# Audio tower on one core: second feed-forward with its down projection two inner blocks behind gate and up, and the token mixer's score order moved by one

## The reference

```
h = mixer(x)                        # 128 sequences of 512, 32 channels: softmax(q k) v
h = h + attention(layernorm(h))     # a0: rotary positions, 32 heads of 16
h = h + ternary_ffn(layernorm(h))   # f0: silu(x w1) * (x w3), w2, weights in {-s, 0, s}
h = h + attention(layernorm(h))     # a1: alibi slopes, 16 heads of 32
h = h + fp4_ffn(layernorm(h))       # f1, the stage that the change is about
```

```
gate, up = x @ w_gu          # 512 -> 2 x 1408; a scale for each output and 128 inputs
h = silu(gate) * up
y = h @ w_down               # 1408 -> 512
out = y / sqrt(mean(y*y) + 1e-6)
```

## Time and profile before

| | |
|---|---|
| median of 3 runs (lowest to highest) | 2395.11 us (2394.86 to 2395.63) |
| profiled execution: its own time | 2391.57 us |
| its span, first to last instruction | 2389.8 us |
| granted TensorE clock over the span | 0.985 |
| PE busy | 2244.2 us, 94% of the span |
| DVE / ACT / POOL busy | 1662.7 / 1495.3 / 1021.4 us |

### The profile page before, as it was taken

One profiled execution on the slowest core, in us unless ns is written; L12 is line 12 of the kernel. 1 busy time (PEld: TensorE's weight loads), 2 busy tenths in 40 slices (PEclk: granted clock), 3 DMA queues, 4 the chain that ended last, 5 costly groups with the idle time before them and its releaser, 6 DMA issues. The chain is left out here.

```text
span 2389.8 us, 41107 instructions
## 1 busy us (share of the span) xinstructions
PE 2244.2 (94%) x13188; PEld 1128.5 (47%) x13188; DVE 1662.7 (70%) x2931; ACT 1495.3 (63%) x2398; POOL 1021.4 (43%) x1007
## 2 busy tenths in 40 slices
PE   6999999998999996799999999999987999999998
PEld 2333333335666663344444445666652444444443
DVE  6666666665888887456667634666657888888873
ACT  4666666666788785355656425667745666667663
POOL 1222222237777773223324302444434555555552
PEclk9999999999999998799999999999999999999999
DMA  5545445442343211312223212222221011111101
GB/s 146 138 127 135 129 127 135 130 110 66 111 131 114 67 58 36 109 50 79 80 89 93 67 48 84 80 79 79 79 67 40 23 49 40 53 41 45 45 27 53
DMA packets 144300, 194.94 MB, mean 82 GB/s; under 512 B 32773, under 2 KB 76261, under 8 KB 144154
## 3 DMA queue, kind: packets, MB, share of 16 engines
q1 hardware_dynamic: 115642, 154.79, 21.7%
q10 hardware_dynamic: 28512, 38.28, 5.7%
HBM read 125.10 MB, written 42.21 MB: 70 GB/s over the span
## 5 line engine op out<-in xcount | busy, mean ns | idle before, releaser
L341 DVE TENSOR_REDUCE tm_negmax<-tm_s 128x1 f32<-128x512 f32 x512 | 323.3, 679 | 164.7 <-PE tm_s L384 164.4
L303 ACT ACTIVATE tm_prob<-tm_s 128x1024 f32<-128x1024 f32 x256 | 257.6, 1023 | 136.9 <-PE tm_s L404 130.6
L2119 PE MATMUL f_part<-f_xhi,gu 128*128 128x512 f16 x704 | 269.4, 383 | 17.8 <-ACT f_firstg L1922 6.3
L2119 PE MATMUL f_part<-f_xlo,gu 128*128 128x512 f16 x704 | 268.6, 382 | 0.0
L421 PE MATMUL tm_o<-tm_prob,tm_vt 128*64 128x512 f32 x1024 | 255.7, 620 | 0.0
L1888 POOL TENSOR_TENSOR f_firstg<-f_firstg,f_secondg 128x512 f32<-128x512 f32 x88 | 150.7, 1712 | 193.3 <-DVE f_secondg L2006 193.3
L2141 PE MATMUL f_pz<-dn,f_ghi 128*128 128x512 f16 x704 | 214.5, 380 | 5.9 <-ACT f_zc L1954 5.9
L384 PE MATMUL tm_s<-tm_qk 96*128 96x512 f16 x512 | 199.2, 391 | 14.6 <-DMA tm_qk<-tm_xs 14.1
L264 POOL TENSOR_TENSOR tm_hn<-tm_nd,tm_rows 128x1024 f32<-128x1024 f32 x32 | 75.3, 2353 | 291.8 <-DMA tm_rows<-rden 291.8
L404 PE MATMUL tm_s<-tm_qk 98*128 98x512 f16 x512 | 194.2, 382 | 1.6 <-DMA tm_qk<-tm_mrow 1.6
L975 PE MATMUL a_bankB<-a_wo,a_yThi 128*128 128x512 f16 x512 | 158.7, 393 | 4.1 <-DVE a_yTlo L899 4.0
(11 more groups left out here) (190 smaller groups left out, 5668.4 us busy)
## 6 DMA issues: line engine op xcount, KB each, us to landing
tm_qk<-tm_xs SPq DMA_DIRECT2D x384, 64.0 KB, 2.1
tm_xqk<-in_qk ACTq DMA_DIRECT2D x32, 512.0 KB, 4.3
a_hin<-h SPq DMA_DIRECT2D x64, 256.0 KB, 2.7
a_hres<-h SPq DMA_DIRECT2D x64, 256.0 KB, 3.0
h<-a_hout SPq DMA_DIRECT2D x64, 256.0 KB, 2.5
f_hin<-h SPq DMA_DIRECT2D x64, 256.0 KB, 2.7
f_hres<-h SPq DMA_DIRECT2D x64, 256.0 KB, 2.8
tm_vt<-in_vt ACTq DMA_DIRECT2D x32, 256.0 KB, 3.0
```

The source lines that it names most:

```text
L303: nc.scalar.activation(prob[b][:, 2 * h:2 * h + 2, :], s2[:, i % 2, :, :], ACT.Exp, scale=SCALE).then_inc(exp_done, 1)
L341: nc.vector.tensor_reduce(negmax[u][:, m:m + 1], s1[:, p % BANKS, :], AX.X, ALU.max, negate=True).then_inc(s1_read, 1)
L2119: last = nc.tensor.matmul(part[q % BANKS][:, :], (gate, up)[which][:, j, m * P:(m + 1) * P], xparts[x][u][:, j, :], start=x == 0, stop=x == 1)
```

## The change

In the second feed-forward the down projection of a block runs two blocks behind it (`LAG = 2`), in the same step, with its 12 matmuls spread one and two at a time behind the 8 products. Four sums, one for each tile of the group, stay open in four PSUM banks (`pz` becomes a list). Products and transposes share the other four banks in turn (`turn`, `bank_of`, `wait_bank`) where there were six and one. `ghi` and `glo` become rings of 4 blocks. The last two blocks of a group are projected in the first two blocks of the next step, so there are 9 steps where there were 10. The four sums are copied out together in blocks 1 and 2. `hidden` and `hidden_lo` of a group's last block move into the next step's first block.

The float16 halves of `xn` are made before the transposes: ACT `x_high`, POOL `x_low`, then PE makes 8 float16 transposes into one bank, and one ACT copy (`copy_x`, 1024 float16 values a partition) takes both halves out. DVE's `x_lo` goes. In the mixer `LEAD` becomes 15, and the transposes move by one use of the banks, so that one more matmul for maxima stands between the eighth maximum and the transpose that needs it.

The core of the diff (the renaming of arguments, the loops that call `step_u`, and what only follows from these are left out):

```diff
-    LEAD = 14
+    LEAD = 15
-        return 0 if m == 0 else m + 1 if m < 9 else m + 2
+        return m if m < 2 else m + 1 if m < 10 else m + 2
-        return 1 if pair else 10
+        return 2 if pair else 11
...
-    BANKS = 6
-    xn = sb("xn", [P, DM], F32)
-    xhi, xlo = pair("xhi", [P, KT, GT], F16), pair("xlo", [P, KT, GT], F16)
+    xn, halves = sb("xn", [P, DM], F32), sb("halves", [P, 2, DM], F16)
+    xs = pair("xs", [P, 2, KT, GT], F16)
     act_out, prod = pair("act_out", [P, GT], F32), pair("prod", [P, GT], F32)
-    ghi, glo = pair("ghi", [P, MT, GT], F16), pair("glo", [P, MT, GT], F16)
+    RING = 4
+    ghi, glo = sb("ghi", [P, RING, GT], F16), sb("glo", [P, RING, GT], F16)
-    zc, square = [extra_sb(f"zc{i}", [P, DM], F32) for i in range(2)], extra_sb("square", [P, DM], F32)
+    zc, square = [extra_sb(f"zc{i}", [P, DM], F32) for i in range(NT)], extra_sb("square", [P, DM], F32)
-    part5, pz, px = (ps(n, [P, GT], F32) for n in ("part5", "pz", "px"))
-    part = [ps(f"part{i}", [P, GT], F32) for i in range(BANKS - 1)] + [part5]
+    bank = [ps(f"bank{i}", [P, GT], F32) for i in range(8)]
+    turn = [bank[i] for i in (3, 4, 5, 2)]
+    pz = [bank[i] for i in (6, 7, 0, 1)]
+    pz_free = [before.done[n] for n in ("y_done", "y_done", "yTlo_done", "out_done")]
...
-    down_to = {0: (0, 0, 6), 1: (0, 6, 12), 2: (0, 12, 18), 3: (0, 18, 23), 4: (0, 23, 28), 5: (0, 28, 33),
...
-    out_at = {9: (1, 0), 14: (1, 1), 20: (1, 2), 3: (2, 3)}
+    squares_at = [3, 5, 7, 8]
+    mean_at = [4, 6, 8, 9]
+    out_at = [5, 7, 9, 10]
+    LAG = 2
+    uses = []
+    for m in range(MT):
+        uses += [(m, i) for i in range(8)]
+        if m in norm_at:
+            uses.append((None, norm_at.index(m)))
+    assert len(uses) % 4 == 0
+    def bank_of(m, i):
+        return turn[uses.index((m, i)) % 4]
+    def wait_bank(pe, g, m, i):
+        at = len(uses) * g + uses.index((m, i)) - 4
+        if at >= 0 and uses[at % len(uses)][0] is None and at // len(uses) == GROUPS - 1:
+            at -= 4
+        if at < 0:
+            return
+        back, (m, i) = at // len(uses), uses[at % len(uses)]
+        if m is None:
+            pe.wait_ge(s["xs_done"], NT * (back + 1) + i + 1)
+        else:
+            pe.wait_ge(s[("scale_done", "join_done")[i % 2]], 4 * (MT * back + m) + i // 2 + 1)
...
-        def step(k, u):
-            n = 2 * k + u
-            store(n - 2, 2)
+        def step(n):
             residual(n - 1, 0)
-            store(n - 2, 3)
             residual(n - 1, 1)
             load(n + 1, 2)
             load(n + 1, 3)
@@ -1856,6 +1878,8 @@
             store(n - 1, 1)
             residual(n - 1, 3)
             load(n + 2, 1)
+            store(n - 1, 2)
+            store(n - 1, 3)
         return normalise, step
...
+        def x_low(g, i):
+            if inside(g, GROUPS):
+                t = NT * g + i
+                wait(pool, s["high_done"], t + 1)
+                wait(pool, s["xT_ready"], t)
+                pool.tensor_tensor(halves[:, 1, :], xn[:, :], halves[:, 0, :], ALU.subtract).then_inc(s["low_done"], 1)
...
+            if i >= 0:
+                x_low(0, i)
...
+                sum_parts(n, m, 0)
+                if m + 1 in norm_at:
+                    x_low(n + 1, norm_at.index(m + 1))
+                if m in mean_at:
+                    inverse_rms(n - 1, mean_at.index(m))
+                sum_parts(n, m, 1)
                 if m + 3 in norm_at:
                     inverse_deviation(n + 1, norm_at.index(m + 3))
...
         def normalise(i):
-            x_hi(0, i, 0)
-        def scale_part(g, m, u, which, j):
+            if i:
+                copy_x(0, i - 1, 0)
+            if i < NT:
+                x_high(0, i)
...
+        def hidden_hi(g, m):
+            if inside(g, GROUPS):
+                n = MT * g + m
+                wait(act, s["prod_done"], n + 1)
+                wait(act, s["part_ready"], 8 * (n - 1))
+                nc.scalar.copy(ghi[:, n % RING, :], prod[n % 2][:, :]).then_inc(s["ghi_done"], 1)
+        def x_high(g, i):
+            if inside(g, GROUPS):
+                t = NT * g + i
+                wait(act, s["xn_done"], t + 1)
+                wait(act, s["xT_ready"], t)
+                nc.scalar.copy(halves[:, 0, :], xn[:, :]).then_inc(s["high_done"], 1)
+        def copy_x(g, i, u):
+            if inside(g, GROUPS):
+                px = (bank_of(None, i) if g else turn[3])[:, :].bitcast(F16)
                 wait(act, s["xT_ready"], NT * g + i + 1)
                 if i == 0:
                     wait(act, s["part_ready"], 8 * MT * (g - 1))
-                nc.scalar.copy(xhi[u][:, :, i * P:(i + 1) * P], px[:, :].rearrange("p (j n) -> p j n", j=KT))\
-                    .then_inc(s["xhi_done"], 1)
+                nc.scalar.copy(xs[u][:, :, :, i * P:(i + 1) * P].rearrange("p x j n -> p (x j) n"),
+                               px.rearrange("p (n c) -> p n c", c=P)).then_inc(s["xs_done"], 1)
...
-                wait(act, s["out_done"], t - 1)
-                nc.scalar.copy(zc[i % 2][:, :], pz[:, :]).then_inc(s["zc_done"], 1)
+                wait(act, s["out_done"], t + 1 - NT)
+                nc.scalar.copy(zc[i][:, :], pz[i][:, :]).then_inc(s["zc_done"], 1)
...
-        def step(k, u):
-            n = 2 * k + u
+        def step(n):
             for m in range(MT):
-                for which in range(2):
-                    at = 2 * m + which
-                    if at in copied_at:
-                        back, i = copied_at[at]
-                        z_out(n - back, i)
-                    scale_part(n, m, u, which, 0)
-                    if at in copied_at:
-                        squares(n - back, i)
-                    scale_part(n, m, u, which, 2)
-                    if which == 0 and m:
-                        hidden_hi(n, m - 1, u)
-                gate_act(n, m, u)
-                if m in norm_at:
-                    x_hi(n + 1, norm_at.index(m), 1 - u)
-            z_out(n - 1, 3)
-            squares(n - 1, 3)
-            hidden_hi(n, MT - 1, u)
+                if m - 1 in norm_at:
+                    copy_x(n + 1, norm_at.index(m - 1), (n + 1) % 2)
+                scale_part(n, m, 0, 0)
+                if m == LAG:
+                    z_out(n - 1, 3)
+                scale_part(n, m, 0, 2)
+                hidden_hi(*((n, m - 1) if m else (n - 1, MT - 1)))
+                if m == LAG - 1:
+                    z_out(n - 1, 0)
+                scale_part(n, m, 1, 0)
+                if m == LAG - 1:
+                    z_out(n - 1, 1)
+                if m + 1 in norm_at:
+                    x_high(n + 1, norm_at.index(m + 1))
+                if m in squares_at:
+                    squares(n - 1, squares_at.index(m))
+                scale_part(n, m, 1, 2)
+                if m == LAG - 1:
+                    z_out(n - 1, 2)
+                gate_act(n, m)
...
-                wait(dve, s["xT_ready"], t)
+                wait(dve, s["low_done"], t)
-        def x_lo(g, i, u):
-            if inside(g, GROUPS):
-                wait(dve, s["xhi_done"], NT * g + i + 1)
-                nc.vector.tensor_tensor(xlo[u][:, :, i * P:(i + 1) * P], px[:, :].rearrange("p (j n) -> p j n", j=KT),
-                                        xhi[u][:, :, i * P:(i + 1) * P], ALU.subtract).then_inc(s["xlo_done"], 1)
...
+                before = (n, m - 1) if m else (n - 1, MT - 1)
+                join_part(n, m, 0, 1)
+                hidden(*before)
+                join_part(n, m, 0, 3)
+                hidden_lo(*before)
+                if m in mean_at:
+                    mean_square(n - 1, mean_at.index(m))
+                join_part(n, m, 1, 1)
+                if m + 2 in norm_at:
+                    x_normalised(n + 1, norm_at.index(m + 2))
+                join_part(n, m, 1, 3)
+                if m in out_at:
+                    output(n - 1, out_at.index(m))
                 if m + 3 in norm_at:
-                    i = norm_at.index(m + 3)
-                    row_stats(n + 1, i, 2 * (n + 1) + i // 2)
-            hidden(n, MT - 1, u)
-            hidden_lo(n, MT - 1, u)
+                    row_stats(n + 1, norm_at.index(m + 3))
...
+        def products_of(g, m, which, j):
+            if inside(g, GROUPS):
+                i = 4 * which + j
+                if m == 0 and i == 0:
+                    wait(pe, s["xs_done"], NT * (g + 1))
+                wait_bank(pe, g, m, i)
+                for x in range(2):
+                    last = nc.tensor.matmul(bank_of(m, i)[:, :], (gate, up)[which][:, j, m * P:(m + 1) * P],
+                                            xs[g % 2][:, x, j, :], start=x == 0, stop=x == 1)
+                last.then_inc(s["part_ready"], 1)
+        def transpose_x(g, i):
+            if inside(g, GROUPS):
+                t = NT * g + i
+                px = (bank_of(None, i) if g else turn[3])[:, :].bitcast(F16)
+                wait(pe, s["low_done"], t + 1)
```

(43 more changed lines are left out.)

159 lines of the change are left out of this document (52 added, 107 removed), and 3 rows, old and new, of the table down_to.

## The result

The changed kernel takes 2355.93 us (median of 4 runs, 2354.9 to 2361.06) where the kernel before, beside it, takes 2395.14: a ratio of 0.984, 95% interval 0.9823 to 0.9857. Its profiled execution took 2356.43 us, with a span of 2354.5. From profile to profile that is 35.3 us of span, from median to median 39.2: the profiled execution of before lay 3.6 us under its median, this one 0.5 over its own. TensorE's granted clock over the span is 0.985 in both.

The account below looks back on a forecast made before the run. PE was taken to bound the kernel, idle 38.4 us in the second feed-forward. Terms -28.4 (PE idle), +4.9 (tail), -2.3 (before first product), -6.5 (mixer) sum to -32.3 off the 2395.11 median: 2362.8 us, own range 2354 to 2371, overall 2347 to 2382.

Parts of the forecast that it names:

- PE's idle time in the stage: Second feed-forward: PE's idle time goes from 38.4 to 5 + 3 + 2 = 10 us, 28.4 us less.
- margins of half a microsecond in a dozen places aren't all kept: Bank margins in the second feed-forward's steps: 3 us of PE stalls in all, with 0 and 25 as ends.
- The end of a step: Full steps: DVE waits 1.43 us before the last block's product; 1.9 us in each of 6 steps, 11.3 in all.
- Step 0 and the drain: Second feed-forward: about 24 us idle in step 0, 2.8 between step 8's sums; blocks 0 and 1 keep some 5.
- Before the first product: Attention's last steps: without `x_lo`, about 1.2 us earlier in each of two rounds; 2.3 us less, ends +3 and -4.
- The tail: Last copy to the end: 6.7 us becomes 11.6, 4.9 us more, with outputs 2 and 3 waiting for fetched rows.
- The mixer: Matmul behind the transpose starts 0.11 us earlier for each of 60-odd transposes, limited by three banks: 6.5 us less.
- `x_low` on POOL hidden: POOL's added subtraction, 1.04 us a tile, stays hidden unless DVE's slack is gone; if every one blocked DVE, 29 us worse.
- 8 to 25 us: Rival: four banks and a busier POOL cost PE this much; time 2371 to 2388, chance 0.20.
- neutral: Rival: stalls near 1.1 us in each block with an `x_low`; chance 0.03.
- slower: Rival: POOL's subtraction and inverse delay the second sum, `hidden` and DVE's joins; up to 64 us, 2424, chance 0.05.
- The mixer's whole wait: Rival: the bank is free earlier than read, winning 64 x 0.46 = 29 us instead of 6.5; 2340, chance 0.07.

Follow-up runs that it names:

- e8: The changed kernel with three PSUM banks in turn instead of four for the gate and up products and the steps' transposes: 2358.47 us, one run.
- e4: The changed kernel with POOL's low-half subtraction done twice, the first time into a tile nobody reads: ratio 0.9922 to the kernel before.
- e10: The changed kernel with the last block's product and halves back at the step's end in DVE's and ACT's order: 2369.91 us, one run.
- e3: The changed kernel with halves made the old way (float32 transposes, low half subtracted from PSUM by DVE): ratio 0.9983 to the kernel before.
- e1: The kernel before with only the mixer's part of the change (LEAD 15 and the use numbers that follow): ratio 0.9973 to the kernel before.
- e5: The changed kernel with four buffers each for fetched rows and outputs, and the last step's mean squares one place earlier on DVE: ratio 0.9841 to the kernel before.
- e6: The changed kernel with the mixer's transposes of maxima behind their slot's scores instead of ahead, with the bank order that follows: ratio 0.9782 to the kernel before.
- b2: The changed kernel with e5 and e6, and the second pair's maxima ahead of the fourth sequence's stacking in SP's queue: ratio 0.9842 to the kernel before.

## Why the prediction was right, point by point

2362.8 us was forecast, 2355.93 came, within the forecast's own range. The mechanism was the one predicted. The sum of -32.3 came out as -35.3 from profile to profile; the other 3.9 us of the miss are the step from the profiled execution to the median, which was taken over from the kernel before. That the sum is so near is partly luck: its four terms came to -37.3, 5.0 us more than forecast, and 2.1 us of that went again in two stretches that the change does not touch. These terms were mis-sized:

- **PE's idle time in the stage: 28.4 us less predicted, 31.4 measured.** What is left is 550.7 - 0.2 - 543.5 = 7.0 us where I had 10. Blocks 0 and 1 cost 4.5 (first joins at 1793.27 and 1804.69, 11.4 apart, less 6.9 of work; predicted 5), the last low half 1.9 (predicted 2), stalls 0.6 (predicted 3). The step that was off is "margins of half a microsecond in a dozen places aren't all kept": they are all kept, and e8 and e4 show some 0.7 us of room from two sides. The margin was read nearly right, and a cost put on it nevertheless.
- **The end of a step.** The 1.9 us a step were put down to DVE's wait before the last block's product. e10 brings wait and time back, by the order on DVE and ACT together; in its trace it is ACT's scale, behind the high half, that PE waits for.
- **Step 0 and the drain.** The larger part of the gain. It is read from the counts and windows of the two profiles, and e10 against the kernel before gives it 19.0 us, with the full steps as long as they were.
- **Before the first product: 2.3 us predicted, 5.5 measured, outside the ends of +3 and -4.** I had read 1.2 us in each of two rounds. The last four outputs of the attention lie 8.4, 10.0 and 7.1 us apart now, and 11.8, 10.7 and 9.9 before: 3.3, 0.7 and 2.8 us in three rounds, 6.8 in all. The waits for `x_hi` had been 3.4, 3.0 and 4.1 us, and I took too little of them as lying on the attention's path. Against that, it is 5.1 us from the attention's last output to the first product now and was 3.8, which gives 1.3 back. The new chain from the transposes at 1786.04 to the product is 5.3 us, where I had 5.8. e3 shows that the gain belongs to the halves. How much of it is clock is open: e1, with the old code, has 75.4 us to the first join where before and e3 have 77.1, so some 1.7 us can vary by itself. All of that lies in the first of the three rounds (10.1 us in e1, 11.8 before and in e3), the one where the change gains 3.3.
- **The tail: 4.9 us predicted, 5.8 measured.** Outputs 2 and 3 start 6.2 and 8.0 us behind the last copy, where I had 6.2 and 7.05. The second fetch left at 2346.74: the second output stands 1.5 us behind the first, not 0.8, since its mean square waits in DVE's queue behind the first output. That I had left out; e5 moves it. It explains half of what the last output is late; the other half is the fetch, whose rows were used 3.3 us after it left, where I had 2.8.
- **The mixer: 6.5 us predicted, 6.2 measured,** by the bank arithmetic to the hundredth. Only 3.3 us of it are left behind the handover in this profile, with the lower clock there; whether that belongs to the change is open (see e1).
- **`x_low` on POOL hidden.** It takes 1.15 us where I had 1.04, and next to none of it reaches the path in the steps; of a second one 0.46 us does (e4). The 29 us of the prediction did not come, but not because DVE and POOL leave each other alone. From 1861 to 2335 us of the kernel before, `f_hout`, which reads two tiles of SBUF, takes 1.76 us in the 13 cases where a POOL sum started ahead of it and 0.74 in the 13 others; POOL's `f_firstu` sum takes 1.27 us otherwise and 1.71 where `f_hout` started first. In the same stretch of the change, the only DVE instructions that run beside an `x_low` are joins, which read only one of their two tiles from SBUF, and row statistics, which read one tile; they take their usual 0.75 and 0.68 us:

```profile
2025.39 1.16 POOL L1902 TENSOR_TENSOR f_halves<-f_xn,f_halves 128x512 f16<-128x512 f32 x1
2025.63 0.75 DVE L2049 SCALAR_TENSOR_TENSOR f_secondu<-f_bank,f_factor,f_secondu 128x512 f32<-128x512 f32 x1 [0.60 <-ACT f_secondu L1958]
2026.30 0.68 DVE L2073 BATCH_NORM_STATS2 f_stats<-f_hin 128x6 f32<-128x512 f32 x1
```

  The rule of the Trainium skill ("SBUF — State Buffer", "Who interferes with whom") that the prediction named, by which an instruction of DVE with two SBUF inputs contends with a reading one of GpSimd, agrees with these rows: it had nothing to act on at this place of the order. The outputs gained from their new place: in this stretch all 27 take 0.74 us.
- **The rivals.** PE waits for neither `f_firstu` nor `f_secondu` in the steps. The signs came nearly as named: steps 1 to 6 of 67.9 and 68.26 us, a mixer tile of 16.04, 0.18 us before the matmul behind the transpose instead of 0.3, and the last projection 7.7 us behind the last product instead of 6. "8 to 25 us", "neutral" and "slower" are out, though the chain of "slower" is real and 0.7 us away. The mixer's whole wait was not won, but 14 us more of it was to be had by another order (e6).

## What to carry to other kernels

When a wait ends, ask which buffer the next instruction takes: one slot further ahead won 0.1 us a burst, and moving the transpose past one product, so that each takes the bank that is free first, won 0.33 in the burst (14 us in all, after what the later maxima cost), without any more memory. A wait in a shared queue costs what stands behind it: the largest mis-sized term was DVE standing before a subtraction with another stage's instructions queued behind, and the 1.9 us a step were two queues' order. A margin read from the profile is worth a test by one bank less or one operation more before it is priced; and a transfer moved up in a queue pushes something else back, as b2 showed. Before an instruction is moved to another engine, look at what will run beside it: whether a collision costs anything is read from the durations in the trace, with and without the neighbour.

## What the runs showed of the hardware that I had not expected

- TensorE's granted clock at the handovers differs between runs with the same instructions up to there, by chance or with the part of the program that is not the same (see e1). It is 1.00 (2.4 GHz) in a busy stretch, and where PE has been idle the mean of a stretch lies between that and 0.5 (1.2 GHz). In the stretch around the first product (1779 to 1820 us) e1 has 0.88 and the change 0.96 (e1 makes the halves in the old way there; e5, with the instructions of the change, has 0.93):

```profile
1779.00:1820.00 41.00, 29.89 (x124) 11.58 (x122) 25.75 (x46) 19.34 (x31) 13.43 (x11) 0.88 0.10 33
```

```profile
1779.00:1820.00 41.00, 32.84 (x173) 14.76 (x172) 26.78 (x46) 24.67 (x37) 17.67 (x16) 0.96 0.13 39
```

  From the mixer's end to the ninth row statistics, the same instructions take 58.2 us in e1 and 61.1 in the change. The runs of the kernel before lie between 2386.5 and 2396.71 us; how much of that is the clock can't be told from the runs without a profile, but the spread hides gains of 2 to 3 us.
- ACT's copy of 128x1024 float16 values from PSUM took 1.01 us, the same as its float32 exponentials of that size (1.02): it got no cheaper with float16.
- VectorE and GpSimd hold each other up, by who starts first: 0.74 us becomes 1.76 for `f_hout`, 1.27 becomes 1.71 for POOL's sum, and a VectorE join that reads PSUM takes 0.75 either way.
